# The bias of the output projection: four transposes of a repeated column in place of a matmul with one row

## The chip, the cores and the metric

The kernel runs on one core of one Trainium2 chip. The metric is the device time of one execution in microseconds (us), lower is better. The kernel before ran three times: 2654.74, 2656.70 and 2658.29 us, median 2656.7 us. A further execution was recorded by the hardware profiler; all rows below are from it.

## What is computed

Four sequences of 1024 rows with 1024 features go through a selective state-space layer and then through a feed-forward layer with routed experts. In short, all in float32:

```python
# state space: x is layer-normed and is the gate z; ctx goes in
x_in  = einsum('ed,bld->bel', in_proj_w, ctx)          # 1024 x 512 weights
u     = silu(causal_conv4(x_in) + conv_b)
dt_lo, Bm, Cm = split(einsum('ke,bel->bkl', x_proj_w, u))   # 32, 16, 16 rows
delta = softplus(dt_proj_w @ dt_lo + dt_proj_b)
state = state * exp(delta * A) + (delta * u) * Bm      # 16 states a channel, over 1024 steps
y     = (sum over states of state * Cm + D * u) * silu(z)
x     = x + y.T
# feed-forward, on the layer-normed x (called xn)
gate, top = top_k(softmax(xn.flatten() @ switch_w.T + switch_b), 2)
o   = sum over the 2 experts of gate * (gelu(xn_head @ w1 + b1) @ w2 + b2)
x   = x + (xn + o) @ w3.T + b3
```

The change is about the last line's `+ b3`, a vector of 1024 values that is added to every row.

## The kernel before, in words

**Stages.** The channels are cut in J = 8 blocks of P = 128, the time in TH = 2 halves of T = 512. One step of the scan is one block of channels over one half: 16 steps a batch (the names use g for the step), and each step has eight slots of two states. In a slot ScalarE makes dA = exp(delta * A) (L1100), VectorE multiplies du by B (L1299) and scans the two states (L1326) into one of three pairs of h buffers, GpSimd multiplies them with C (L799), and TensorE adds the products up by eight transposes into the bank yT (L862, `sum_pair`). Four more transposes of u * D open that sum (L957), four transpose the gate's block (L944, "zT"), the four matmuls of in_proj make the input ten steps ahead (L833), x_proj comes twice a batch (L845), and L854 makes the input of the softplus.

**What sets the order.** Each engine has a program of its own, written out from one table: `Schedule` holds for batch b and slot t the extra pieces of work. The feed-forward layer of batch b - 1 is done while batch b is scanned: its logits (L976), the transposes of the rows (L905), the experts (L918, L928), and the output tiles. The last batch's feed-forward part has nothing beside it and makes the tail.

**Output tiles.** An output tile is 128 rows by QD = 512 features: 16 tiles a batch (two halves uu of the rows, two halves dh of the features, four row blocks k), 64 in all. In the scan a tile is four "tile" pieces (part 0 to 3) of two blocks of the contraction each, put in slots 56 to 79 and 99 to 126 of the batch behind; within a slot they follow `sum_pair`. In the tail the 16 tiles stand one behind the other. Before part 0, TensorE waits until the bank (one of two, F0 and F1, in turn) was read out, and then writes the bias into it; then it waits for its share of w3 and adds the eight blocks (L995). The float32 matmul of 128x512 appears as two passes in the trace. VectorE adds the residual while it reads the bank (L1285), and SyncE stores the tile (L708) and loads the next residual (L701).

**The bias before.** At setup b3 is loaded as one row of 1024 values into partition B3 = 64 of the tile dtw (L555), whose partitions 0 to 32 hold dt_proj and its bias, and 96 to 127 hold rows of B and C. For a tile, one matmul multiplies row 64 of a tile of ones (1 x 128) by 512 values of that row (1 x 512), with start=True (L991). The loads of the small constants are thirteen DMAs on SyncE's queue (L559), all counted on one semaphore; ScalarE and GpSimd wait for it before their first work, TensorE before x_proj.

Of the kernel before, what the change touches and what calls it, by code (L numbers as in the profile page):

```python
# [11 lines left out]
P = 128  # L12
# [4 lines left out]
J = DI // P  # L17
# [10 lines left out]
SWL = DI // SD  # L28
QD = 512
NQ = DI // QD  # L30
B3 = 64
RA = 4
RH = 3
SLOTS = PAIRS
# [215 lines left out]
def build(nc, x, ctxT, w_inT, conv_w, conv_b, x_projT, dt_projT, dt_b, A_log, D, sw, sw_b,  # L250
# [4 lines left out]
    with ExitStack() as ctx:  # L255
        def sb(name, shape, dt=F32):
            return ctx.enter_context(nc.sbuf_tensor(name, shape, dt))
# [11 lines left out]
        ident = sb("ident", [P, P])  # L269
        ones = sb("ones", [P, P])  # L270
# [4 lines left out]
        dtw = sb("dtw", [P, DI])  # L275
# [3 lines left out]
        Av = sb("Av", [P, J * N])  # L279
        b1c = sb("b1c", [P, E])  # L280
        b2c = sb("b2c", [P, E])
        swb = sb("swb", [P, E])

        ctxs = sb("ctxs", [P, DK, T])
# [62 lines left out]
        dense = ctx.enter_context(nc.psum_tensor("dense", [P, 8, T], F32))  # L347
# [89 lines left out]
        def bank_of(b, *name):  # L437
            return PLAN.use[(b, *name)][0]

        def count(b, *name):  # L440

            return PLAN.use[(b, *name)][1]
# [19 lines left out]
        def f_index(b, k):  # L462
            return 2 * TB * b + k

        def logit_batch(b, k):
            return b - 1 if k >= TB else b
# [4 lines left out]
        def sw_tile(b, k, i):  # L471

            m = SWL * (k % TB) + i
            if k < TB:
                return ring_b[m % RING_B], sw_b_loaded[m % RING_B], 1 + 16 * (b * len(range(m % RING_B, SWL * TB, RING_B)) + m // RING_B + 1)
            if b < NB:
                r = m % RING_A
                return ring_a[r], sw_a_loaded[r], 1 + 16 * ((b - 1) * len(range(r, SWL * TB, RING_A)) + m // RING_A + 1)
            return ring_t[m % RING_T], sw_t_loaded[m % RING_T], 1 + 16 * (m // RING_T + 1)
# [4 lines left out]
        def row_of(b, what, k):  # L484

            if (b, what, k) in PLAN.fill:
                i = PLAN.fill[(b, what, k)]
                return row[:, i % 2, :], row_loaded[i % 2], 1 + 16 * (i // 2 + 1)
            i = k - TB - 2 if what == "logits" else 2 + k
            return tail_rows[i], tail_row_loaded[i], 1 + 16  # L490
# [18 lines left out]
        def w3_of(b, uu, dh, c):  # L509
            if b < NB:  # L510
                return w3h, w3_loaded[c], 1 + 16 * (2 * NQ * (b - 1) + NQ * uu + dh + 1)
            if dh == 0:
                return w3h, w3_loaded[c], 1 + 16 * (2 * NQ * (b - 1) + 1)
            return w3_tail, w3_tail_loaded[c], 1 + 16

        @block.sync
        def _(sync):
            e = sync
# [24 lines left out]
            with nc.allow_non_contiguous_dma(reason="small weights, once"):  # L543
                for dst, src in (
                    (cw[:], conv_w.rearrange("(j p) k -> p j k", p=P)),
                    (cb[:], conv_b.rearrange("(j p) -> p j", p=P)),
                    (xpw[:], x_projT.rearrange("(j p) k -> p j k", p=P)),
                    (Dv[:], D.rearrange("(j p) -> p j", p=P)),
                    (Av[:].rearrange("p (j n) -> p j n", n=N), A_log.rearrange("(j p) n -> p j n", p=P)),
                    (b1c[0:HD], b1.rearrange("e f -> f e")),  # L550
                    (b1c[HD:P], b1.rearrange("e f -> f e")),
                    (b2c[0:HD], b2.rearrange("e d -> d e")),
                    (b2c[HD:P], b2.rearrange("e d -> d e")),
                    (swb[:], sw_b.partition_broadcast(P)),
                    (dtw[B3:B3 + 1], b3.rearrange("(o d) -> o d", o=1)),  # L555
                    (dtw[0:DR], dt_projT),
                    (dtw[DR:DR + 1], dt_b),
                ):
                    e.dma_start(dst, src).then_inc(const_loaded, 16)  # L559
# [264 lines left out]
        def _(pe):  # L824
            e = pe
# [54 lines left out]
            def slot(b, t):  # L880
                st, q = divmod(t, SLOTS)
                g, c = STEPS * b + st, TH * b + st // J
                th, j = divmod(st, J)
                for what, *a in PLAN.slots[b][t]:
# [8 lines left out]
                    elif what == "turn":  # L893
                        uu, k, i = a
                        bank = bank_of(b, *name)
# [7 lines left out]
                        for n in range(J // 2):  # L903
                            d = (J // 2) * i + n
                            mm = e.transpose(dense[:, bank, n * P:(n + 1) * P], rows[:, d * P:(d + 1) * P], ident[:])  # L905
                        mm.then_inc(tr_done, 1)
                    elif what == "hidden":
# [7 lines left out]
                        for i in (0, 1):  # L915
                            bank = bank_of(b, *name, i)
# [3 lines left out]
                    elif what == "expert_out":  # L920
                        uu, hp = a
                        bank = bank_of(b, *name)
# [4 lines left out]
                        for i in (0, 1):  # L927
                            mm = e.matmul(dense[HD * i:HD * i + HD, bank, :], w2s[:], hs_of(b, hp)[:, i, :],  # L928
                                          start=True, stop=True)
# [21 lines left out]
                if b < NB:  # L951
                    if q == 2:
# [3 lines left out]
                        for k in range(TB):  # L956
                            e.matmul(yT[:, k, :], uD[:, k * P:(k + 1) * P], ident[:], is_transpose=True,  # L957
                                     start=(k == 0), stop=False, skip_group_check=True)
# [3 lines left out]
                for what, *a in PLAN.slots[b][t]:  # L962
                    if what == "logit":
                        k, i = a
                        f = f_index(logit_batch(b, k), k)
                        first = k % TB == 0 and i == 0
                        if i == 0:
                            e.wait_ge(norm_done, 1 + f + 1)
                        if first:
                            e.wait_ge(evac[F2], 1 + count(b, "logits", k // TB))  # L970
                        weights, loaded, value = sw_tile(b, k, i)
                        e.wait_ge(loaded, value)
                        rows = row_of(b, "logits", k)[0]
                        for n in range(SD // 32):
                            lo = i * SD + 32 * n
                            mm = e.matmul(dense[32 * n:32 * n + 32, F2, 0:32 * E], rows[:, lo:lo + 32],  # L976
                                          weights[:, :, 32 * n:32 * n + 32],
                                          start=first, stop=(k % TB == TB - 1 and i == SWL - 1))
                        mm.then_inc(sw_used, 1)
                    elif what == "tile":  # L980


                        uu, dh, k, part = a
                        bank = bank_of(b, "tile", uu, dh, k)
                        w3, loaded, value = w3_of(b, uu, dh, part)
                        if part == 0:
                            if dh == 0 and k == 0:
                                last = ("expert_out", uu, J - 1)
                                e.wait_ge(evac[bank_of(b, *last)], 1 + count(b, *last) + 1)
                            e.wait_ge(evac[bank], 1 + count(b, "tile", uu, dh, k))  # L990
                            e.matmul(dense[:, bank, :], ones[B3:B3 + 1, :], dtw[B3:B3 + 1, dh * QD:(dh + 1) * QD],  # L991
                                     start=True, stop=False)
                        e.wait_ge(loaded, value)
                        for d in range(J // W3C * part, J // W3C * (part + 1)):
                            mm = e.matmul(dense[:, bank, :], xT_of(b, uu)[:, d, k * P:(k + 1) * P], w3[:, d, :],  # L995
                                          start=False, stop=(d == J - 1))
                        mm.then_inc(part_done, 1)
            turns(slot)

        @block.scalar  # L1000
# [443 lines left out]
```

## Time and profile before

| | |
|---|---|
| runs shown, us | 2654.74, 2656.70, 2658.29 |
| profiled execution, us | 2655.29 |
| its span, us | 2653.5 |
| mean granted TensorE clock | 0.849 of 2.4 GHz |
| TensorE matmul (PE) busy | 1998.5 us, 75% |
| TensorE weight load (PEld) busy | 1083.4 us, 41% |
| VectorE (DVE) busy | 2238.3 us, 84% |
| ScalarE (ACT) busy | 1542.8 us, 58% |
| GpSimd (POOL) busy | 1446.2 us, 55% |

The span is the profiled part of the execution; 1.8 us lie around it. Engines run at the same time, each through its own list, and wait for each other by semaphores. PE and PEld overlap: the weights of the next pass are loaded while the present one runs. Durations of matmuls overlap their successors in the record, since passes are pipelined; what a pass costs is therefore read from the start of one group to the start of the next, and not from its length. A busy share is an average over stages with different limits.

### The profile page before, as it was taken

How to read it: one execution, taken by the hardware profiler on the slowest of the kernel's cores; microseconds unless marked ns; L12 is line 12 of the kernel's file. 1: busy time of each engine (PE TensorE's matmuls, PEld its weight loads, DVE VectorE, ACT ScalarE, POOL GpSimd, SP SyncE). 2: the span in 40 equal slices, each digit the busy share in tenths (PEclk: the TensorE clock that was granted, in tenths of full speed). 3: DMA queues.
4: the chain of work that ended last, by engine and by line, in shares of the span. 5: the costliest groups of instructions: out<-in, count | busy, mean ns of one | idle time of the engine just before them, and what ended most of it. 6: DMA issues, size and time to landing. Idle time of an engine off the chain costs nothing.

```text
span 2653.5 us, 29890 instructions
## 1 busy us (share of the span) xinstructions
PE 1998.5 (75%) x9360; PEld 1083.4 (41%) x9360; DVE 2238.3 (84%) x2928; ACT 1542.8 (58%) x2225; POOL 1446.2 (55%) x990
## 2 busy tenths in 40 slices
PE   5365566666676898899675798899675797895899
PEld 2143334443443344344443344344443344442233
DVE  4399999999999889998999889998999999994300
ACT  2366555555666757855676746954666858852400
POOL 0177666666765556555775555555675666662000
PEclk9677777778787899899787899899787998997899
DMA  3401241445552364466461274465560274557311
GB/s 107 179 27 59 73 164 49 158 159 191 183 182 72 112 222 135 135 210 199 160 226 67 89 242 140 127 197 191 181 223 26 78 231 146 170 184 267 150 57 62
DMA packets 200050, 386.78 MB, mean 146 GB/s; under 512 B 30642, under 2 KB 96178, under 8 KB 199892
## 3 DMA queue, kind: packets, MB, share of 16 engines
q1 hardware_dynamic: 199892, 384.87, 43.3%
q8 instruction: 75, 1.23, 0.2%
q14 instruction: 83, 0.68, 0.1%
HBM read 350.73 MB, written 34.08 MB: 145 GB/s over the span
## 4 chain that ended last, share of the span: by engine, by line
PE 37%; issue 22%; DVE 22%; ACT 9%; POOL 6%; DMA 1%; SPq 1%; DVEq 0%; ACTq 0%; POOLq 0%
PE dense L995 13%; DVE h L1326 10%; PE dense L862 8%; PE dense L833 5%; POOL h L799 5%; DVE dense L1299 5%; ACT dA L1100 3%; DVE u L1191 2%; PE dense L845 2%; PE dense L991 2%; PE dense L928 2%; PE dense L976 2%; PE dense L918 1%; ACT L1059 1%; ACT hs L1162 1%
## 5 line engine op out<-in xcount | busy, mean ns | idle before, releaser
L799 POOL TENSOR_TENSOR h<-h,Cb 128x1024 f32<-128x1024 f32 x512 | 1208.0, 2359 | 473.6 <-DVE h L1326 450.0
L1100 ACT ACTIVATE dA<-delta,Av 128x512 f32<-128x512 f32 x1024 | 702.9, 717 | 514.0 <-DVE h L1326 511.9
L862 PE MATMUL dense<-ident,h 128*128 128x128 f32 x4096 | 635.1, 310 | 274.4 <-POOL h L799 272.9
L862 PEld LDWEIGHTS dense<-ident,h 128*128 128x128 f32 x4096 | 545.4, 161 | 450.0 <-POOL h L799 353.8
L1326 DVE TENSOR_TENSOR_SCAN h<-dA,state,dense 128x512 f32<-128x512 f32 x512 | 628.1, 1264 | 56.1 <-PE dense L862 33.8
L1299 DVE TENSOR_TENSOR dense<-dense,Bb 128x512 f32<-128x512 f32 x1024 | 653.3, 684 | 4.2 <-ACT dense L1055 2.1
L1326 DVE TENSOR_TENSOR_SCAN h<-dA,dense 128x512 f32<-128x512 f32 x512 | 597.6, 1204 | 24.0 <-PE dense L862 11.3
L995 PE MATMUL dense<-w3h,xT 128*128 128x512 f32 x832 | 391.6, 604 | 0.0
L833 PE MATMUL dense<-ctxs,win 128*128 128x512 f32 x512 | 273.0, 684 | 31.2 <-DMA win<-in_w_inT 25.4
L854 PE MATMUL dense<-dtaug,dtw 33*128 33x512 f32 x128 | 104.1, 906 | 209.8 <-DVE u L1191 180.5
L793 POOL COPY state<-h 128x2 f32<-128x2 f32 x256 | 48.0, 188 | 382.0 <-DVE h L1326 380.5
L995 PEld LDWEIGHTS dense<-w3h,xT 128*128 128x128 f32 x832 | 146.9, 191 | 167.1 <-issue 167.1
L833 PEld LDWEIGHTS dense<-ctxs,win 128*128 128x128 f32 x512 | 110.8, 227 | 169.0 <-issue 138.4
L1191 DVE SCALAR_TENSOR_TENSOR u<-dense,cw,u 128x511 f32<-128x511 f32 (+2 forms) x192 | 140.5, 732 | 32.2 <-ACT u L1025 16.1
L1285 DVE TENSOR_TENSOR res<-dense,res 128x512 f32<-128x512 f32 x64 | 43.8, 685 | 122.8 <-PE dense L995 122.5
L1059 ACT ACT_TABLE_LOAD x112 | 143.7, 1283 | 2.0
L1055 ACT COPY dense<-du_s 128x512 f32<-128x512 f32 x64 | 37.6, 587 | 155.3 <-DVE dense L1299 133.3
L976 PE MATMUL dense<-sww,row 128*32 128x256 f32 x1336 | 115.3, 433 | 15.5 <-ACT row L1130 14.6
L854 PEld LDWEIGHTS dense<-dtaug,dtw 33*128 33x128 f32 x128 | 25.7, 250 | 240.9 <-issue 240.9
L928 PE MATMUL dense<-hs,w2s 128*64 128x512 f32 x224 | 74.6, 731 | 38.5 <-ACT hs L1162 38.2
L786 POOL TENSOR_TENSOR xt<-szT,xt 128x512 f32<-128x512 f32 x64 | 81.8, 1278 | 3.0 <-DVE szT L1243 3.0
L1162 ACT ACT_TABLE_LOAD x49 | 62.9, 1283 | 34.4 <-PE dense L918 34.0
(136 smaller groups left out, 1842.1 us busy)
## 6 DMA issues: line engine op xcount, KB each, us to landing
sww<-in_sw SPq DMA_DIRECT2D x170, 512.0 KB, 4.4
Bb<-bc_scratch SPq DMA_DIRECT2D x64, 512.0 KB, 4.5
Cb<-bc_scratch SPq DMA_DIRECT2D x64, 512.0 KB, 5.8
w3h<-in_sw SPq DMA_DIRECT2D x56, 512.0 KB, 7.5
w3h<-in_w3T SPq DMA_DIRECT2D x52, 512.0 KB, 4.7
row<-x_scratch SPq DMA_DIRECT2D x42, 512.0 KB, 4.7
win<-in_w_inT SPq DMA_DIRECT2D x64, 256.0 KB, 4.0
row<-in_x SPq DMA_DIRECT2D x32, 512.0 KB, 4.3
```

Of the source, the lines that this page charges most:

```text
L799: e.tensor_tensor(h[:, s:s + 2, :], h[:, s:s + 2, :], Cb[:, 2 * q:2 * q + 2, :], ALU.mult).then_inc(prod_done, 1)
L833: mm = e.matmul(dense[:, bank, :], win[:, par, k, :], ctxs[:, k, :], start=(k == 0), stop=(k == DK - 1))
L854: e.matmul(dense[:, S, :], dtw[0:DR + 1, j * P:(j + 1) * P], dtaug[:], start=True, stop=True) \
L862: mm = e.matmul(yT[:, k, :], h[:, 2 * (q % RH) + i, k * P:(k + 1) * P], ident[:], is_transpose=True, start=False, stop=(q == PAIRS - 1 and ...
L928: mm = e.matmul(dense[HD * i:HD * i + HD, bank, :], w2s[:], hs_of(b, hp)[:, i, :], start=True, stop=True)
L976: mm = e.matmul(dense[32 * n:32 * n + 32, F2, 0:32 * E], rows[:, lo:lo + 32], weights[:, :, 32 * n:32 * n + 32], start=first, stop=(k % TB ...
L995: mm = e.matmul(dense[:, bank, :], xT_of(b, uu)[:, d, k * P:(k + 1) * P], w3[:, d, :], start=False, stop=(d == J - 1))
L1059: e.preload_act_table_set("natural_log_exp_and_others")
L1100: e.activation(dst, delta[:, st % 2, :], ACT.Exp, scale=Av[:, j * N + n:j * N + n + 1]).then_inc(dA_done, 1)
L1191: i = e.scalar_tensor_tensor(out=u[:, G % UR, s:T], in0=dense[:, bank, 0:T - s], scalar=cw[:, j, k:k + 1], in1=u[:, G % UR, s:T], op0=ALU. ...
L1299: e.tensor_tensor(duB[:, n % 2, :], du[:], Bb[:, n, :], ALU.mult).then_inc(duB_done, 1)
L1326: e.tensor_tensor_scan(h[:, 2 * (q % RH) + n % 2, :], decay, inflow, state[:, j * N + n:j * N + n + 1] if th else 0.0, ALU.mult, ALU.add) \
```

## The change

The row of b3 in dtw goes, and with it the constant B3. In its place a new tile b3c [128, 8] holds b3 by columns: partition p of column j is b3[128 j + p]. For a tile, TensorE now makes four transposes: column 4 dh + n, repeated 128 times along the free dimension, is the stationary operand, the identity is the moving one, and the result, 128 features in every one of the 128 rows, goes to columns 128 n to 128 n + 127 of the bank. The first has start=True; the others, and the matmuls of w3 behind them, add to the same bank.

```diff
-B3 = 64
...
+        b3c = sb("b3c", [P, J])
...
-                    (dtw[B3:B3 + 1], b3.rearrange("(o d) -> o d", o=1)),
+                    (b3c[:], b3.rearrange("(j p) -> p j", p=P)),
...
                             e.wait_ge(evac[bank], 1 + count(b, "tile", uu, dh, k))
-                            e.matmul(dense[:, bank, :], ones[B3:B3 + 1, :], dtw[B3:B3 + 1, dh * QD:(dh + 1) * QD],
-                                     start=True, stop=False)
+                            for n in range(QD // P):
+                                column = QD // P * dh + n
+                                e.matmul(dense[:, bank, n * P:(n + 1) * P], b3c[:, column:column + 1].broadcast_to([P, P]),
+                                         ident[:], is_transpose=True, start=(n == 0), stop=False, skip_group_check=True)
                         e.wait_ge(loaded, value)
                         for d in range(J // W3C * part, J // W3C * (part + 1)):
                             mm = e.matmul(dense[:, bank, :], xT_of(b, uu)[:, d, k * P:(k + 1) * P], w3[:, d, :],
-                                          start=False, stop=(d == J - 1))
+                                          start=False, stop=(d == J - 1), skip_group_check=True)
```

## Rows read from the trace of the kernel before

**Rows 1.** Page, part 4: the chain that ended last, shares of the span by line
```profile
PE dense L995 13%; DVE h L1326 10%; PE dense L862 8%; PE dense L833 5%; POOL h L799 5%; DVE dense L1299 5%; ACT dA L1100 3%; DVE u L1191 2%; PE dense L845 2%; PE dense L991 2%; PE dense L928 2%; PE dense L976 2%; PE dense L918 1%; ACT L1059
```
**Rows 2.** Busy time by stretch; x is instructions, first numbers are start:end and length
```profile
core 0: us, PE busy (x) PEld busy (x) DVE busy (x) ACT busy (x) POOL busy (x), PEclk, DMA share, GB/s
916.00:1030.00 114.00, 107.92 (x413) 57.99 (x412) 100.08 (x126) 61.91 (x92) 65.44 (x38) 0.97 0.57 191
1118.00:1240.00 122.00, 121.02 (x577) 58.72 (x576) 106.93 (x134) 65.74 (x98) 72.35 (x41) 1.00 0.57 182
1522.00:1634.00 112.00, 105.93 (x403) 56.91 (x403) 98.28 (x123) 59.95 (x88) 63.78 (x37) 0.97 0.58 193
1722.00:1844.00 122.00, 121.01 (x577) 58.87 (x577) 106.95 (x134) 65.74 (x98) 72.41 (x41) 1.00 0.57 182
2112.00:2206.00 94.00, 89.00 (x356) 47.83 (x354) 86.41 (x102) 55.79 (x79) 60.20 (x36) 1.00 0.62 202
2309.00:2412.00 103.00, 96.58 (x489) 48.72 (x487) 99.64 (x121) 52.88 (x73) 67.46 (x33) 0.99 0.52 168
2520.00:2653.50 133.50, 130.22 (x290) 52.00 (x288) 11.82 (x17) 0.00 (x0) 0.00 (x0) 1.00 0.17 59
```
**Rows 3.** Timeline of the tail, TensorE: start us, us, engine, line, operands
```profile
2617.69 1.12 PE L991 MATMUL dense<-dtw,ones 1*128 1x512 f32 x2
2618.74 7.13 PE L995 MATMUL dense<-Cb,u 128*128 128x512 f32 x16
2625.81 1.12 PE L991 MATMUL dense<-dtw,ones 1*128 1x512 f32 x2
```
**Rows 4.** Timeline of a tile stretch of batch 1, TensorE
```profile
957.85 3.60 PE L995 MATMUL dense<-w3h,xT 128*128 128x512 f32 x8
961.28 1.04 PE L862 MATMUL dense<-ident,h 128*128 128x128 f32 x8
962.25 1.12 PE L991 MATMUL dense<-dtw,ones 1*128 1x512 f32 x2
963.30 3.70 PE L995 MATMUL dense<-w3h,xT 128*128 128x512 f32 x8
966.93 1.12 PE L854 MATMUL dense<-dtaug,dtw 33*128 33x512 f32 x2
...
978.15 0.60 PE L944 MATMUL dense<-ident,xz 128*128 128x128 f32 x4
978.58 1.04 PE L862 MATMUL dense<-ident,h 128*128 128x128 f32 x8
```
**Rows 5.** VectorE's waits from 1118 to 1240 us: us in total, times, longest
```profile
DVE h L1326 <- ACT dA L1100: 6.5, 1, 6.5
DVE h L1326 <- PE dense L862: 5.9, 3, 3.0
DVE delta L1221 <- ACT delta L1049: 2.4, 1, 2.4
```
**Rows 6.** Timeline of the setup, SyncE's issues
```profile
11.05 0.87 SPq L559 DMA_DIRECT2D cb<-in_conv_b  x1
20.51 0.34 SPq L559 DMA_DIRECT2D dtw<-in_b  x1
```
**Rows 7.** Groups by line and form: busy us, mean ns, idle before
```profile
L1299 DVE TENSOR_TENSOR dense<-dense,Bb 128x512 f32<-128x512 f32 x1024 | 653.3, 684 | 4.2 <-ACT dense L1055 2.1
L944 PE MATMUL dense<-ident,xz 128*128 128x128 f32 x256 | 41.4, 285 | 21.2 <-DVE delta L1221 20.4
L944 PEld LDWEIGHTS dense<-ident,xz 128*128 128x128 f32 x256 | 28.2, 143 | 44.0 <-issue 43.9
L1389 DVE TENSOR_TENSOR sww<-hs,hot 128x512 f32<-128x512 f32 x12 | 8.3, 692 | 0.7
```
**Rows 8.** Busy time by stretch, as rows 2: a slow stretch, then lone transposes
```profile
942.50:949.20 6.70, 6.62 (x15) 3.31 (x15) 6.57 (x9) 4.11 (x7) 6.17 (x6) 0.57 1.03 373
...
2473.58:2478.33 4.75, 4.75 (x24) 3.65 (x24) 3.84 (x18) 3.26 (x7) 0.00 (x0) 0.64 0.98 366
2478.54:2479.73 1.19, 1.19 (x8) 0.81 (x8) 1.15 (x2) 0.94 (x2) 0.00 (x0) 1.00 1.03 399
```

## The prediction

> **What bounds the kernel now.** I start with the chain of waits of the whole span [rows 1]. Its shares by line put TensorE's w3 products (L995) first with 13%, then VectorE's scan (L1326), and the bias matmul L991 itself holds 2%. Two per cent of 2653.5 us is some 53 us; one bias costs 1.05 us from its start to that of the next matmul [rows 3], so about 50 of the 64 lie on the chain. That is why I look at the places of L991 and not at its busy share.
>
> The second view is the table by stretch [rows 2]: the six stretches of the scan in which output tiles are made (two in each of the batches 1, 2 and 3), and the tail from 2520 us on. The reader is to compare PE's and DVE's busy time with the length. In the tail PE is busy 130.2 of 133.5 us and DVE 11.8: PE is the bound alone. In the four stretches of batches 1 and 2 PE has 107.9 of 114 us, 121.0 of 122, 105.9 of 112 and 121.0 of 122, while DVE, which sets the pace of a scan without tiles, is idle for 13.9, 15.1, 13.7 and 15.1 us. So there too PE is mostly the bound. In batch 3 PE has 89.0 of 94 us with 7.6 us of idle DVE, and then 96.6 of 103 with only 3.4. ACT and POOL have room everywhere.
>
> The third view says whom DVE waits for in one such stretch [rows 5]: 5.9 us for L862 (TensorE's sum of a pair, which frees an h buffer), and 6.5 and 2.4 us for ScalarE's dA and delta. ScalarE's turn comes behind x_proj (L845) and the product L854, both on TensorE, so these waits too are at least in part PE's lateness, one engine further on.
>
> **What the change removes.** At each of 64 tiles one matmul with one row of contraction, which the trace shows as two passes (L991 x2). In the tail a tile repeats every 2625.81 - 2617.69 = 8.12 us [rows 3]. Without a bias its 16 passes would take 16 x 0.429 = 6.86 us; the 0.429 is read where nothing of the kind stands around: L995 x8 from 957.85 to 961.28 is 3.43 us [rows 4]. So the bias costs 8.12 - 6.86 = 1.26 us, which is more than the 1.05 from its own start to the next: the seam shows as well before it (L862 x8 takes 0.97 us when L991 follows, 961.28 to 962.25) and behind it (L995 x8 then takes 3.63 instead of 3.43, of which a part is due to the L854 that follows) [rows 4].
>
> **What it adds on TensorE.** Four transposes of 128 columns into the same bank, weights first, just as L862, L944 and L957 do. Four of L944 between L995 and L862 take 978.58 - 978.15 = 0.43 us [rows 4], and L995 ahead of them and L862 behind show no seam. All this at the full clock. So the sum for a tile is 1.26 - 0.43 = 0.83 us less on PE.
>
> That the weights are one column read 128 times has no row on TensorE. The bounds: nothing extra, which gives the 0.43; or the weight load no longer hides behind the product before it, 143 + 285 = 428 ns each [rows 7], 1.71 us for four, which is 0.45 us more than now. A gain over the 0.43 I exclude, since the number of columns is the same. The nearest row is of another engine: DVE's multiply by a broadcast operand (L1389) takes 692 ns against 684 for one with plain operands (L1299) [rows 7]. I take nothing extra.
>
> **Setup.** The load of b3 as one row had an issue of 0.34 us; b3c has the shape and the pattern of cb, whose issue took 0.87 us [rows 6]. Two more loads of the same group come behind it on SP, then the rows and the next w_in tiles, and ACT, POOL and (for x_proj) PE wait for the whole group. All are delayed by 0.53 us, and nothing covers it, because ACT's first tap stands behind that wait. The bounds are 0 (the issue overlaps with landings) and some 1.5 us (the issue, and 1024 small elements on the way, which I guess at twice the issue's difference). I take 0.5 us.
>
> **What it moves.** No instruction changes its order: four transposes stand where the matmul stood, on PE, and the same waits (evac of the bank, w3_loaded) stand ahead of them or behind. The DVE, ACT and POOL lists are untouched. The 0.8 us earlier end of a tile wakes DVE's L1285 and SP's store, and in the tail these have room: DVE is busy 11.8 of 133.5 us.
>
> **Sum, tail.** 16 tiles x 0.83 = 13.3 us, all on the path.
>
> **Sum, scan.** 48 tiles, eight in a stretch: at most 8 x 0.83 = 6.6 us a stretch. DVE's idle time caps it, since DVE can't be shortened otherwise: 6.6 us is below 13.9, 15.1, 13.7, 15.1 and 7.6; in the last stretch the cap is 3.4, and as TensorE has 6.4 us to spare there I count 1.4. That is 5 x 6.6 + 1.4 = 34.4 us at most. At least it is 0, if ACT and POOL set the same waits. Between these I choose two thirds, 23 us: PE is full in the stretches, which speaks for the whole; but over half of the waits in [rows 5] (8.9 of 14.8 us) end on ScalarE, whose own work between PE and DVE doesn't shrink, and a wait gives back only what was gained since the one before it.
>
> **The result.** 13.3 + 23 - 0.5 = 35.8 us off the profiled execution's 2655.3 us gives 2619.5. The median of the runs shown, 2656.7, is 1.4 us above that execution, so I give 2621 us.
>
> **A rule against it.** Of 32 transposes that stood alone at 2473.58 to 2479.73 us, with no other matmul among them, the first 24 ran at a mean granted clock of 0.64 and the last 8 at 1.00 [rows 8], so the clock rose to 2.4 GHz while TensorE did nothing but transposes. And the tile stretches, full of L862's transposes, have 0.97 to 1.00 [rows 2]. The Trainium skill, "TensorE: Matmul & The Clock Gate", Part 4 (PE-mode transpose), says the contrary: the full clock doesn't engage for transpose mode, as it doesn't count as PE-busy in the same way. By that rule the kernel would get more uncounted work and could lose clock (second rival); by the row it can't.
>
> **Rivals.**
> 1. *Tail only.* The scan's waits are set by others too (dA by ScalarE, delta by its chain), and end as late as before: 2655.3 - 13.3 + 0.5 = 2642.5, 2644 against the median. For it: the 8.9 us in [rows 5]. Against: L991 is on the chain some 50 times, when the tail has 16.
> 2. *The clock falls, slower.* In the tail, the transposes would break the run of multiplying passes 16 times, and TensorE would drop to 1.2 GHz. Where the clock was down, 942.5 to 949.2 us, it was 0.57 [rows 8], that is almost all at 1.2 GHz, and there everything on PE takes twice as long. The tail without the bias matmul is 16 x 7.29 = 117 us at the full clock; each tenth of it at the lower level costs 11.7 us, so from three tenths the whole gain is gone, and with all of it at 1.2 GHz the time is 2621 + 117 = 2738. Against: rows 8 and 2 as above.
> 3. *The weight load of a repeated column is in the open, slower.* 0.45 us more a tile instead of 0.83 less: 7.2 in the tail, two thirds of 21.6 in the scan, 0.5 in the setup: 22 us, 2679 against the median. It decides from 0.83 / 4 = 0.21 us of extra time for each load.
> 4. *No gain.* The seams of rows 4 come from something else than the single row (the first product into a bank, say) and stand around the transposes as well: each seam of some 0.2 us on both sides and between the passes takes back the most of 0.83; about 2655.
>
> **Chances.** Forecast 0.64, reaching from all of the scan's 34.4 us (2609.5) to a third of them (2632.4); tail only 0.20 (2644); no gain 0.07; slow load 0.05; clock 0.04. The range from 2609 to 2645 holds the first two. About 0.2%, 5.3 us, is what a measurement of this kernel can tell from no change. Faster by more: the first two cases and a little of the fourth, 0.85. Within it: 0.06. Slower: 0.09.
>
> **What would show it.** In the changed kernel's timeline of the tail a tile should repeat every 7.29 us, with four transposes in 0.43 us, and L995 in 3.43 us per eight passes with no seam; clock 1.00. Each tile stretch should be shorter by 4 to 5 us and DVE's idle time in it smaller by as much, the named waits for L862 first. The first scan should start 0.5 us later. A tail period near 8.1 or above, a PEld time for the new line over 0.2 us, or a granted clock under 0.95 in the tail would each refute a step, and unchanged stretches with a shorter tail would make it rival 1.

## The result, and the profile after

The changed kernel took 2620.5 us in the median of four runs (2614.8 to 2621.0), the kernel before 2656.1 (2654.7 to 2658.3, four runs): ratio 0.986, 95% interval 0.9843 to 0.9877. Run again on another chip beside thirteen runs of the kernel before it gave 0.9862 (0.9825 to 0.9900), 2616.7 against 2654.1 us, with single runs from 2610.4 to 2625.8 (the kernel before beside it: 2643.8 to 2658.5). The forecast was 2621. Two executions of one experiment below (the delayed kernel before), at 3012 and 9517 us, were in a slow state of the chip and are left out of its ratio.

The chain of waits of the changed kernel, where L993 is the new bias and L997 the w3 products (answers to [rows 1]):

```profile
DVE h L1328 12%; PE dense L997 11%; PE dense L862 7%; POOL h L799 5%; DVE dense L1301 5%; PE dense L833 4%; ACT dA L1102 3%; DVE u L1193 3%; PE dense L845 2%; PE dense L928 1%; ACT L1061 1%; PE dense L918 1%; DVE szT L1245 1%; PE dense L976
```

The w3 products have given up the first place to VectorE's scan, and of the bias no line is left among the large ones.

The timeline of the tail, TensorE (start us, us; answers to [rows 3]):

```profile
2595.03 0.60 PE L993 MATMUL dense<-ident,b3c 128*128 128x128 f32 x4
2595.46 7.03 PE L997 MATMUL dense<-Cb,u 128*128 128x512 f32 x16
2602.33 0.60 PE L993 MATMUL dense<-ident,b3c 128*128 128x128 f32 x4
```

A tile repeats after 2602.33 - 2595.03 = 7.30 us; the four transposes take 0.43 us from start to start and the 16 passes 6.87. The seams are gone. The same in a tile stretch of batch 1 (answers to [rows 4]):

```profile
951.61 3.60 PE L997 MATMUL dense<-w3h,xT 128*128 128x512 f32 x8
955.04 1.04 PE L862 MATMUL dense<-ident,h 128*128 128x128 f32 x8
955.92 0.60 PE L993 MATMUL dense<-ident,b3c 128*128 128x128 f32 x4
956.35 3.60 PE L997 MATMUL dense<-w3h,xT 128*128 128x512 f32 x8
```

L862 ahead of the bias now takes 0.88 us in place of 0.97, and the bias 0.43 in place of 1.05.

The weight load of the repeated column, from the groups by line and form (busy us, mean ns; answers to [rows 7]):

```profile
L993 PE MATMUL dense<-ident,b3c 128*128 128x128 f32 x256 | 38.9, 275 | 0.0
L944 PEld LDWEIGHTS dense<-ident,xz 128*128 128x128 f32 x256 | 28.5, 144 | 44.0 <-issue 43.8
L993 PEld LDWEIGHTS dense<-ident,b3c 128*128 128x128 f32 x256 | 30.5, 138 | 13.8 <-issue 13.8
```

138 ns for the repeated column and 144 for a plain tile: repetition costs nothing.

**Where the time went.** The first start of L957 marks each step of the scan, so the two profiled executions can be laid side by side, in us. Steps 7 to 11 hold the first tile stretch of a batch, steps 12 to 15 the second; what stands behind L957 of the last step is called the rest, and the 16 tiles are in it.

| stretch | before | after | difference |
|---|---|---|---|
| to the first step | 118.58 | 121.69 | +3.11 |
| batch 0 (no tiles) | 547.12 | 542.64 | -4.48 |
| batch 1, steps 0 to 6 | 257.34 | 255.00 | -2.34 |
| batch 1, steps 7 to 11, tiles | 193.88 | 188.13 | -5.75 |
| batch 1, steps 12 to 15, tiles | 153.40 | 152.20 | -1.20 |
| batch 2, steps 0 to 6 | 256.93 | 248.15 | -8.78 |
| batch 2, steps 7 to 11, tiles | 193.85 | 187.85 | -6.00 |
| batch 2, steps 12 to 15, tiles | 153.39 | 152.11 | -1.28 |
| batch 3, steps 0 to 6 | 245.68 | 248.40 | +2.72 |
| batch 3, steps 7 to 11, tiles | 170.63 | 168.32 | -2.31 |
| batch 3, steps 12 to 14, tiles | 97.67 | 96.21 | -1.46 |
| the rest, 16 tiles in it | 265.00 | 252.34 | -12.66 |
| span | 2653.47 | 2613.04 | -40.43 |

The tile stretches give 18.0 us and the tail 12.7. The other rows sum to -9.8, and the largest of them, 8.8 us, stands in a stretch that holds not one output tile. That was the open question. (Batch 0's 4.5 us are scatter: over the profiles of all the kernels below it takes 542.6 to 543.0 us in four and 545.8 to 547.5 in ten, with either bias in both groups.) Three of its rows in the busy time by stretch, of the kernel before:

```profile
core 0: us, PE busy (x) PEld busy (x) DVE busy (x) ACT busy (x) POOL busy (x), PEclk, DMA share, GB/s
1116.92:1270.32 153.40, 140.06 (x650) 69.55 (x649) 137.51 (x170) 82.27 (x123) 89.77 (x51) 0.96 0.59 191
1270.32:1527.25 256.93, 180.72 (x960) 108.16 (x960) 245.01 (x340) 176.25 (x257) 162.34 (x134) 0.79 0.39 137
1527.25:1721.10 193.85, 166.38 (x736) 86.85 (x734) 175.76 (x221) 133.51 (x184) 109.12 (x60) 0.92 0.53 171
```

and of the changed kernel:

```profile
1107.46:1259.66 152.20, 136.25 (x666) 71.90 (x665) 137.57 (x170) 82.22 (x123) 89.73 (x51) 0.94 0.60 193
1259.66:1507.81 248.15, 171.43 (x961) 102.39 (x961) 243.90 (x339) 176.37 (x256) 162.44 (x134) 0.83 0.40 140
1507.81:1695.66 187.85, 157.18 (x749) 88.16 (x747) 175.33 (x221) 133.47 (x184) 109.23 (x60) 0.94 0.55 178
```

In the middle rows the work is the same (DVE 245.0 and 243.9 us), but TensorE's mean clock is 0.79 in the one and 0.83 in the other.

**Why the second tile stretch gives little.** VectorE's waits in steps 12 to 15 of batch 1 after the change (us in total, times, longest; answers to [rows 5]):

```profile
DVE h L1328 <- ACT dA L1102: 6.0, 1, 6.0
DVE h L1328 <- PE dense L862: 3.1, 2, 1.9
DVE res L1287 <- PE dense L997: 2.7, 1, 2.7
DVE delta L1223 <- ACT delta L1051: 1.6, 1, 1.6
```

L862 fell from 5.9 to 3.1, delta from 2.4 to 1.6 and dA from 6.5 to 6.0 against [rows 5]: 4.1 us gone. But a wait is new: VectorE comes to its turn of adding the residual of the last tile 2.7 us before the tile is through. By steps, 12 to 14 take 110.4 us in place of 114.4, the 4 us that I had expected, and step 15 takes 41.8 in place of 39.0. In step 15 TensorE's clock fell for 6.8 us, 14 us behind its start, where it had stayed up in the kernel before. The same pieces of work in the kernel before and in the changed one:

```profile
1247.50 1.88 PE L995 MATMUL dense<-w3h,xT 128*128 128x512 f32 x4
1249.22 3.60 PE L833 MATMUL dense<-ctxs,win 128*128 128x512 f32 x8
...
1234.88 3.62 PE L997 MATMUL dense<-w3h,xT 128*128 128x512 f32 x4
1238.29 3.86 PE L833 MATMUL dense<-ctxs,win 128*128 128x512 f32 x8
```

and the busy time by stretch there, before and after:

```profile
1245.50:1252.30 6.80, 5.73 (x20) 3.10 (x21) 6.05 (x6) 4.39 (x6) 6.23 (x4) 1.00 0.84 284
1232.00:1238.80 6.80, 5.68 (x13) 3.45 (x14) 6.06 (x6) 4.43 (x6) 6.26 (x4) 0.50 0.95 321
```

At a granted clock of 0.50, which is 1.2 GHz, the four passes take 1238.29 - 1234.88 = 3.41 us in place of 1.72, and the last tile is through 26.9 us behind the start of step 15 in place of 24.1. In batch 2 the same happens more weakly (step 15: 40.7 us in place of 39.0). All seven profiles with transposes in the scan's tiles have it. So in step 15 the clock took back 2.8 and 1.7 us of what the transposes gave. It isn't a matter of transposes: of the kernels below, the one without any bias falls to 1.2 GHz there as well (step 15: 40.7 us), and the one with 128 rows in the bias matmul doesn't (39.0). Nor is a cheaper bias needed: two profiles below with the single row have a longer step 15 in one batch each (the delayed kernels before, 40.3 us in batch 1 and 40.7 in batch 2). Why the clock falls in the one and not in the other was not tried.

The first stretches are not purely the bias either: the kernel with 128 rows gained 4.6 us in steps 7 to 11 of batch 1, more than the 8 x 0.41 = 3.3 us by which its bias is cheaper there.

**Setup.** The new load (answers to [rows 6]):

```profile
20.24 0.43 SPq L559 DMA_DIRECT2D b3c<-in_b  x1
```

Its issue took 0.43 us, 0.09 more than the row's and half of the 0.87 that I had taken from cb. ScalarE's first instruction behind the group started at 24.18 us.

### The profile page after: what moved, and what is told of

It is laid out like the page before. It is cut to its first block, busy times and chain, and to the rows that moved or that the text cites. A ratio compares the mean times of both kernels' runs of the same rounds, so it can differ in the third digit from the quotient of the medians.

```text
span 2613.0 us, 30146 instructions
## 1 busy us (share of the span) xinstructions
PE 1947.3 (75%) x9488; PEld 1099.9 (42%) x9488; DVE 2237.0 (86%) x2928; ACT 1544.3 (59%) x2225; POOL 1446.3 (55%) x990
## 4 chain that ended last, share of the span: by engine, by line
PE 30%; DVE 25%; issue 25%; ACT 9%; POOL 6%; DMA 1%; SPq 1%; DVEq 1%; ACTq 0%; POOLq 0%
DVE h L1328 12%; PE dense L997 11%; PE dense L862 7%; POOL h L799 5%; DVE dense L1301 5%; PE dense L833 4%; ACT dA L1102 3%; DVE u L1193 3%; PE dense L845 2%; PE dense L928 1%; ACT L1061 1%; PE dense L918 1%; DVE szT L1245 1%; PE dense L976 1%; ACT hs L1164 1%
## 5 line engine op out<-in xcount | busy, mean ns | idle before, releaser
L862 PE MATMUL dense<-ident,h 128*128 128x128 f32 x4096 | 651.1, 315 | 280.7 <-POOL h L799 278.5
L862 PEld LDWEIGHTS dense<-ident,h 128*128 128x128 f32 x4096 | 556.6, 164 | 458.2 <-POOL h L799 369.7
L997 PE MATMUL dense<-w3h,xT 128*128 128x512 f32 x832 | 389.3, 601 | 0.0
L833 PE MATMUL dense<-ctxs,win 128*128 128x512 f32 x512 | 267.2, 672 | 31.4 <-DMA win<-in_w_inT 25.0
L854 PE MATMUL dense<-dtaug,dtw 33*128 33x512 f32 x128 | 104.0, 904 | 207.9 <-DVE u L1193 179.1
L997 PEld LDWEIGHTS dense<-w3h,xT 128*128 128x128 f32 x832 | 148.9, 194 | 129.3 <-issue 129.3
L833 PEld LDWEIGHTS dense<-ctxs,win 128*128 128x128 f32 x512 | 108.8, 222 | 165.0 <-issue 138.1
L1287 DVE TENSOR_TENSOR res<-dense,res 128x512 f32<-128x512 f32 x64 | 43.9, 686 | 111.1 <-PE dense L997 110.9
L854 PEld LDWEIGHTS dense<-dtaug,dtw 33*128 33x128 f32 x128 | 25.8, 251 | 239.2 <-issue 239.2
L976 PE MATMUL dense<-sww,row 128*32 128x256 f32 x1336 | 111.2, 420 | 16.1 <-ACT row L1132 16.1
L928 PE MATMUL dense<-hs,w2s 128*64 128x512 f32 x224 | 71.3, 699 | 41.3 <-ACT hs L1164 40.7
L756 POOL TENSOR_TENSOR du_s<-delta,u 128x512 f32<-128x512 f32 x64 | 81.6, 1276 | 1.1 <-DVE delta L1223 1.1
```

What stands on the lines that cost most here:

```text
L833: mm = e.matmul(dense[:, bank, :], win[:, par, k, :], ctxs[:, k, :], start=(k == 0), stop=(k == DK - 1))
L854: e.matmul(dense[:, S, :], dtw[0:DR + 1, j * P:(j + 1) * P], dtaug[:], start=True, stop=True) \
L862: mm = e.matmul(yT[:, k, :], h[:, 2 * (q % RH) + i, k * P:(k + 1) * P], ident[:], is_transpose=True, start=False, stop=(q == PAIRS - 1 and ...
```

## The experiments

**The change again, its two halves, and no bias at all.** All four ran on one chip, beside thirteen runs of the kernel before with a median of 2654.1 us.

*The changed kernel again.*

> The changed kernel once more, as the measure for the others and for its own scatter. Four executions lay at 2614.8, 2620.5, 2620.6 and 2621.0 us. If the scatter comes from where the clock's changes fall against the work, again values from 2614 to 2622 us; if the 2614.8 was a single outlier, all within 1 us of 2620.6.

Four runs: 2618.6, 2625.8, 2614.8 and 2610.4 us. The spread is wider than even the first expectation allowed. Its profiled execution has the same tail (its 16 tiles and what follows take 119.86 us from the first w3 product on, as in the first profile) and the same 248.2 us in steps 0 to 6 of batch 2.

*Transposes in the tail alone, and in the scan alone.* Both loads of b3 stand at setup, so that the two are alike in it. The first has `b == NB` in this place, the second `b < NB`:

```diff
-                            for n in range(QD // P):
-                                column = QD // P * dh + n
-                                e.matmul(dense[:, bank, n * P:(n + 1) * P], b3c[:, column:column + 1].broadcast_to([P, P]),
-                                         ident[:], is_transpose=True, start=(n == 0), stop=False, skip_group_check=True)
+                            if b == NB:
+                                for n in range(QD // P):
+                                    column = QD // P * dh + n
+                                    e.matmul(dense[:, bank, n * P:(n + 1) * P], b3c[:, column:column + 1].broadcast_to([P, P]),
+                                             ident[:], is_transpose=True, start=(n == 0), stop=False, skip_group_check=True)
+                            else:
+                                e.matmul(dense[:, bank, :], ones[B3:B3 + 1, :], dtw[B3:B3 + 1, dh * QD:(dh + 1) * QD],
+                                         start=True, stop=False, skip_group_check=True)
```

> The four transposes in the 16 tiles of the tail alone, the matmul with one row in the 48 tiles of the scan; both loads of b3 at setup. Theory (the path's share as predicted: 13.1 us from the tail, some 23 from the scan): 2656 - 13 + 0.5 = 2643 to 2644 us. Rival (the scan gave little, and the rest of the gain came from elsewhere, such as the other place of the constants or the order of waits): near 2625 us.

> The four transposes in the 48 tiles of the scan alone, the matmul with one row in the tail; both loads of b3. Theory: the tail's period is 8.12 us as before and the whole is 2620.5 + 13 + 0.5 = 2634 us; together with the kernel of the tail alone the two gains add up to that of the change within 3 us. Rival (gains that overlap): the two sum to clearly more or less than 35.5 us.

Tail alone: 2644.9 us, ratio 0.9970 (0.9955 to 0.9985), 9.2 us off. Scan alone: 2631.3 us, ratio 0.9910 (0.9879 to 0.9940), 22.8 us off. Both lie within 3 us of the theory, and the rival (the scan gave little) is out. The two sum to 32.0 us, where the whole change gave 37.4 on that chip: 5.4 us apart, more than the 3 I had allowed, though the intervals are 8 and 16 us wide. The stretches are cleaner than the totals: the tail's 16 tiles and what follows take 132.1 us with the matmul with one row, in the kernel before and in the scan alone, and 119.86 with transposes, 12.2 us less. And steps 0 to 6 of batch 2 take 256.92 us with the tail alone and 248.20 with the scan alone, so 8.7 of the scan's 22.8 us stand where there is no tile.

*No bias.* b3 is left out of the sum:

```diff
-                            for n in range(QD // P):
...
                         for d in range(J // W3C * part, J // W3C * (part + 1)):
                             mm = e.matmul(dense[:, bank, :], xT_of(b, uu)[:, d, k * P:(k + 1) * P], w3[:, d, :],
-                                          start=False, stop=(d == J - 1), skip_group_check=True)
+                                          start=(d == 0), stop=(d == J - 1), skip_group_check=True)
```

> No bias at all: b3 is left out of the sum, the first w3 matmul opens the bank; the load of b3c stays. It prices the four transposes. Theory: the tail's period falls from 7.30 to 16 x 0.429 = 6.86 us, 7 us in all; of the scan's 48 x 0.44 = 21 us about half to two thirds return; 2600 to 2604 us. Rival (in the scan TensorE is no longer the bound once the bias costs 0.43 us, and scans and dA set the pace): only the tail's 7 us, 2613 us.

2614.6 us, only 2.0 below the changed kernel. That is near the rival's number, but not by its sum. The profile's busy time by stretch, batch 2:

```profile
1261.66:1517.79 256.13, 178.90 (x958) 106.30 (x958) 243.79 (x339) 176.16 (x256) 161.89 (x134) 0.79 0.39 136
1517.79:1704.55 186.76, 157.36 (x722) 86.04 (x720) 175.79 (x222) 133.41 (x184) 109.44 (x61) 0.92 0.56 178
1704.55:1855.57 151.02, 133.31 (x634) 68.19 (x633) 138.50 (x171) 82.19 (x123) 89.67 (x51) 0.94 0.60 196
```

The tiles gave a little more: 186.76 and 151.02 us, another 1.1 each below the changed kernel's (some 5 in all six tile stretches, half of what the theory asked for), and the tail's tiles took 113.4 us against 119.9, 6.5 less. But steps 0 to 6 are back at 256.1 us, with the clock at 0.79. Eight microseconds returned in a stretch that the edit doesn't touch.

**Setup.** *Both loads, the second read by nobody.* The kernel before, with the load of b3c added to the group.

> The kernel before with the load of b3c added to the group at setup (14 loads in place of 13), and read by nobody. Theory (the load costs its issue, 0.5 us, once): 2656.5 to 2657 us, the first VectorE tap 0.5 to 0.6 us later. Rival (the first scan step starts 3.1 us later in the profile of the change because of this load): about 2659 us, and the first step again 3 us later.

2656.7 us against 2655.0, ratio 1.0004 (0.9993 to 1.0015), which fits the cost of the issue and is not at odds with no cost. But the interval reaches to 4 us, so it doesn't exclude the rival's 3 either, and that profile did start the first step late, at 122.16 us. *The load behind those of B and C*, with a semaphore of its own:

```diff
-                    (b3c[:], b3.rearrange("(j p) -> p j", p=P)),
...
             load_xz(0, 0, 0)
+            with nc.allow_non_contiguous_dma(reason="small weights, once"):
+                e.dma_start(b3c[:], b3.rearrange("(j p) -> p j", p=P)).then_inc(b3_loaded, 16)
...
+                            if (b, uu, dh, k) == (1, 0, 0, 0):
+                                e.wait_ge(b3_loaded, 1 + 16)
```

> The changed kernel with the load of b3c taken out of the group at setup and issued behind the loads of B and C, with a semaphore of its own for which TensorE waits once before the first output tile. Theory: the setup group is through at 23.3 us or before in place of 24.2, and the whole is 0.5 to 1 us below the changed kernel. Rival (the 3.1 us later first step are the load's doing): 3 us below it.

2619.4 us, ratio 0.9859 (0.9842 to 0.9875). The group is through at 23.31 us, 0.87 before the changed kernel's, but the first step came at 121.76 us, no earlier. The time is the changed kernel's within the spread. What lies between shows in TensorE's first groups of in_proj, here of the kernel before:

```profile
27.10 8.60 PE L833 MATMUL dense<-ctxs,win 128*128 128x512 f32 x16 [2.53 <-DVE u L1191]
54.59 8.52 PE L833 MATMUL dense<-ctxs,win 128*128 128x512 f32 x16 [5.19 <-DMA win<-in_w_inT]
```

of the changed kernel:

```profile
27.72 10.18 PE L833 MATMUL dense<-ctxs,win 128*128 128x512 f32 x16 [3.13 <-DVE u L1193]
57.59 8.92 PE L833 MATMUL dense<-ctxs,win 128*128 128x512 f32 x16 [5.22 <-DMA win<-in_w_inT]
```

and of the one with the late load:

```profile
26.85 8.67 PE L835 MATMUL dense<-ctxs,win 128*128 128x512 f32 x16 [2.49 <-DVE u L1197]
54.53 10.20 PE L835 MATMUL dense<-ctxs,win 128*128 128x512 f32 x16 [5.27 <-DMA win<-in_w_inT]
```

The same 16 passes take 8.5 or 10.2 us, as TensorE's clock came up sooner or later in them, and where the long one falls differs from kernel to kernel.

**What makes the seam.** The kernel before, with 128 rows of contraction in the bias matmul in place of one (a wrong constant takes the place of b3):

```diff
-                            e.matmul(dense[:, bank, :], ones[B3:B3 + 1, :], dtw[B3:B3 + 1, dh * QD:(dh + 1) * QD],
+                            e.matmul(dense[:, bank, :], ones[:], xpw[:].rearrange("p j k -> p (j k)"),
                                      start=True, stop=False)
```

> The kernel before with the bias matmul of 128 rows of contraction in place of one: ones (128x128) times 512 columns of x_proj's weights, so a wrong constant takes the place of b3. Theory (the seams of 0.2 us on either side belong to the matmul with a single row, whose weights are not loaded behind the pass before): the tail's period is 18 x 0.429 = 7.72 us, and the bias costs 0.86 in place of 1.26. Rival (the seams belong to the first pass into a bank): 8.12 us as before.

Its timeline in the tail:

```profile
2615.12 1.02 PE L991 MATMUL dense<-xpw,ones 128*128 128x512 f32 x2
2615.97 7.03 PE L995 MATMUL dense<-Cb,u 128*128 128x512 f32 x16
2622.84 1.02 PE L991 MATMUL dense<-xpw,ones 128*128 128x512 f32 x2
```

The period is 7.72 us and the two passes cost 0.85: the theory, to the hundredth. The matmul with 128 rows, 128 times the work, is 0.40 us cheaper than the one with a single row. One execution took 2635.8 us. By stretches against the kernel before, the tile stretches give 11.7 us in place of the change's 18.0, and the tail's tiles 6.0 in place of 12.2, so some half of the gain of the change is to be had without a transpose.

The single row is not the only shape with seams. L854, with 33 rows, still has them in this kernel:

```profile
1229.91 1.12 PE L854 MATMUL dense<-dtaug,dtw 33*128 33x512 f32 x2
1230.96 1.09 PE L862 MATMUL dense<-ident,h 128*128 128x128 f32 x8
1231.89 1.02 PE L991 MATMUL dense<-xpw,ones 128*128 128x512 f32 x2
1232.75 1.88 PE L995 MATMUL dense<-w3h,xT 128*128 128x512 f32 x4
```

From its start to the next, L854's two passes take 1.05 us, as the single row's did, and the two with 128 rows 0.86. The first part of the seam goes wider still. At the full clock a pass of the w3 products takes 0.43 us to the next start, and 0.52 where one with 33 rows (L854) or one with 128 rows and 32 columns (L976) comes next; a transpose of L862 takes 0.11 us, and 0.20 ahead of L976 or of L918 with its 64 rows. Ahead of the bias with 128 rows nothing is added. So the 0.09 us in front stands where a pass with fewer rows or columns follows a full one, the other parts were seen at 1 and 33 rows, and none of it is special to a single row. How the engine comes to it, by the weight load as the theory has it or otherwise, no run here shows.

**GpSimd adds the bias in the tail.** The late load, transposes in the scan, and in the tail:

```diff
+                    elif what == "tile_out" and b == NB:
+                        uu, dh, k = a
+                        n = part_index(b, uu, dh, k, 0) // W3C
+                        e.wait_ge(b3b_loaded, 1 + 16)
+                        e.wait_ge(res_loaded[n % 2], 1 + 16 * (n // 2 + 1))
+                        e.tensor_tensor(res[:, n % 2], res[:, n % 2], dA[:, dh, :], ALU.add).then_inc(res_biased, 1)
```

dA is free by then and holds b3 repeated over the partitions; VectorE waits for res_biased, and TensorE opens the bank with the first w3 product.

> A version that may beat both: the late load of b3c, the transposes in the scan's tiles, and in the tail no bias on TensorE: GpSimd, idle there, adds a repeated b3 to the residual before VectorE adds the product. Theory: the tail's period is 6.86 us; 16 x 0.43 = 7 us below the kernel with the late load alone, about 2613 us. Rival (the chain load of the residual, GpSimd, VectorE, store, next load becomes longer than two tiles of 13.7 us, or GpSimd slows VectorE): a period of 7.3 us or above and no gain.

2608.75 us, four runs within 1.1 us, ratio 0.9823 (0.9807 to 0.9840). The tiles and what follows take 113.4 us. This is the fastest version: 46 us below the kernel before, about 11 below the late load alone, of which 6.5 us are the tail's tiles. The other microseconds stand mostly (3.9) between the start of the last scan step and the first tile, a piece that took 132.2 us here, 132.5 in the changed kernel and 136.1 with the late load; why it was long there stays open. The chain through GpSimd in its timeline:

```profile
2581.76 1.26 POOL L833 TENSOR_TENSOR res<-res,dA 128x512 f32<-128x512 f32 x1 [5.81 <-DMA res<-x_scratch]
2583.05 0.69 DVE L1306 TENSOR_TENSOR res<-dense,res 128x512 f32<-128x512 f32 x1 [6.17 <-POOL res L833]
2588.65 1.27 POOL L833 TENSOR_TENSOR res<-res,dA 128x512 f32<-128x512 f32 x1 [5.63 <-DMA res<-x_scratch]
2589.91 0.69 DVE L1306 TENSOR_TENSOR res<-dense,res 128x512 f32<-128x512 f32 x1 [6.18 <-POOL res L833]
```

VectorE's turns are 2589.91 - 2583.05 = 6.86 us apart, TensorE's pace, but in these two it is GpSimd's add that ends last (in the next it is the w3 products), so a still shorter tile might meet this chain.

*The same with the load of b3c moved into batch 0's scan:*

> As the kernel with GpSimd's bias in the tail, with the load of b3c moved on from the setup into the first batch's scan (SyncE's slot 100). Theory (the setup lost time wherever this load stood in it): the first scan step begins at 118.6 us as in the kernel before, in place of 120.1 to 121.7, and the whole is 1.5 to 3 us lower, 2606 to 2607 us. Rival (the first step scatters with the clock and not with the load): no difference from 2608.8 us.

2609.9 us (2602.5 to 2613.0), ratio 0.9836 (0.9808 to 0.9863), first step at 120.92 us: the rival. With the group free of the new load the first step began at 118.6 to 121.8 us in seven profiles of this study (before 118.58, late load 121.76, this one 120.92; mean 120.0), with it at 120.7 to 124.1 in six of seven, and at 119.5 in the seventh (the delayed change, below; mean 121.5). These overlap, and the means are 1.5 us apart.

**The eight microseconds in batch 2.** The theory formed after these runs: whether TensorE's clock drops from 2.4 to 1.2 GHz during the expert work of step 5 depends on where the work lies against the clock's changes ahead of it. Two constants' statistics on VectorE, 1.4 us, shift what follows:

```diff
+                if b == 2 and t == 0:
+                    e.wait_ge(const_loaded, 1 + 16 * CONSTS)
+                    e.wait_ge(lgr_done, 4)
+                    for i in (0, 1):
+                        e.bn_stats(lgm[:, i, 0:6], xpw[:].rearrange("p j k -> p (j k)")).then_inc(pad_done, 1)
+                    e.wait_ge(pad_done, 1 + 2)
```

> The kernel before with 1.4 us of needless work on VectorE (two statistics of 512 constants) at the start of batch 2. It only shifts what follows against the times at which TensorE's clock changes. Theory (steps 0 to 6 of batch 2 take 248.2 us where the clock stays at 2.4 GHz during the expert work of step 5, and 255 to 257 us where it drops, and a shift of the start decides): this kernel's steps 0 to 6 of batch 2 take 248 us and the 1.4, in place of 256.9; the whole is 7 us below the kernel before, about 2648 us. Rival (the bias matmuls or their absence in the tiles ahead decide in another way, such as through backlog): 256.9 + 1.4 us, and the whole 1 to 2 us above the kernel before.

> The changed kernel with the same 1.4 us on VectorE at the start of batch 2. Theory: the favourable place is lost, steps 0 to 6 of batch 2 take 255 to 258 us in place of 248.2, and the whole is about 2620 + 8, 2626 to 2630 us. Rival (the transposes themselves keep the clock up): 248.2 + 1.4 us, and 2621 to 2622 us.

The delayed change: 255.67 us in steps 0 to 6 of batch 2 and 2625.1 us in all, ratio 0.9899 (0.9869 to 0.9930), against 0.986 without the delay. 7.5 us came of 1.4, as the theory says; the total is 1 us short of the expected range, and single runs of the changed kernel reach it too (2625.8), so here the stretch says more than the total. The delayed kernel before: 256.21 us, ratio 1.0001 (0.9985 to 1.0017). That is a miss. Its batch 1 had run differently ahead of it (steps 12 to 15 took 155.5 us in place of 153.4), so step 5 fell to another place than planned, with the clock's rise 2.96 us behind its start and not 1.2. The last run put the delay so close that nothing could take the shift back (t == 37 in place of 0):

> The kernel before with the 1.4 us of needless VectorE work put close ahead of step 5 of batch 2 (slot 37), so that nothing between can take the shift back. In the profiles so far the clock's rise nearest to the start of step 5 comes 1.1 to 1.2 us behind it where steps 5 and 6 are short (37.3 and 34.8 us), and 2.0 to 3.0 us behind it where they are long (40.4 to 40.8 and 38.3 to 39.2); in the kernel before it comes 2.6 us behind. Theory (the place alone decides): with the work 1.4 us later the rise comes 1.2 us behind, steps 5 and 6 take 37.3 + 34.8 or near, some 7 us less than before, though the kernel has more work and the bias matmuls of before; the whole near 2649 us in such executions. Rival (the transposes of the tiles ahead are needed): 40.6 + 39.2 us and 2657 us.

Its busy time by stretch in steps 5 and 6, and in 6.5 us within step 5:

```profile
1450.33:1487.74 37.41, 26.10 (x116) 13.13 (x114) 36.61 (x51) 34.62 (x46) 22.84 (x18) 0.86 0.39 141
1487.74:1523.37 35.63, 30.87 (x128) 15.67 (x127) 33.59 (x47) 26.95 (x37) 22.86 (x18) 0.98 0.30 96
1463.40:1469.90 6.50, 6.22 (x27) 3.22 (x28) 6.50 (x9) 6.43 (x8) 5.32 (x6) 1.00 0.07 7
```

The same of the kernel before:

```profile
1460.50:1467.00 6.50, 5.58 (x13) 3.45 (x14) 6.50 (x9) 6.43 (x8) 5.32 (x6) 0.50 0.02 5
...
1447.48:1488.08 40.60, 27.99 (x116) 14.59 (x115) 36.72 (x51) 35.05 (x47) 22.82 (x18) 0.79 0.36 130
1488.08:1527.25 39.17, 34.53 (x129) 17.66 (x128) 33.72 (x47) 26.98 (x38) 22.84 (x18) 0.88 0.26 88
```

13 us behind the start of step 5 the clock is at 1.2 GHz in the kernel before and at 2.4 with the delay, in the same work. Steps 5 and 6 take 37.4 + 35.6 us in place of 40.6 + 39.2: 6.7 us less, near the forecast (37.3 + 34.8). What it does to one piece of work, L833 of that step, before and with the delay:

```profile
1463.18 5.56 PE L833 MATMUL dense<-ctxs,win 128*128 128x512 f32 x8
```

```profile
1464.61 3.60 PE L834 MATMUL dense<-ctxs,win 128*128 128x512 f32 x8
```

The whole kernel, with 1.4 us more to do and the bias matmuls of before, is faster, if by little: 2651.7 against 2655.1 us, ratio 0.9988 (0.9978 to 0.9998). The forecast was near 2649; steps 12 to 15 of the same batch gave back 2.5 us (155.9 in place of 153.4).

## Why the prediction was right, point by point

- **0.83 us a tile, the tail's 13.3 us.** Right: the period went from 8.12 to 7.30 us, which is 13.1 us in 16 tiles. (The 12.2 us of the stretch counted from the first w3 product leave out the first bias.) That the seam belongs to the matmul with one row and not to the first pass into a bank, which I had only read off two places, is shown by the matmul with 128 rows (0.85 us in place of 1.26); the 33 rows of L854 keep it, so it is not a matter of the single row alone.
- **Nothing extra for the repeated column.** Right: 138 ns a load against 144.
- **Two thirds of the scan's 34.4 us, 23.** The tile stretches gave 18.0 us in the profile. This is the term that was too large, by 5 us, and mostly in the second stretches: 1.2 to 1.5 us each where I had expected 4 to 5. In batches 1 and 2 steps 12 to 14 gave 4.0 and 3.0 us, and step 15 took back 2.8 and 1.7, as the clock fell to 1.2 GHz in it and the last tile was late for VectorE's turn at L1287. Without that the term would be about 22.5, an estimate from these steps. The two thirds themselves were a choice between bounds, and no run shows the reason given for them. The first stretches gave 5.8, 6.0 and 2.3.
- **That the total still fitted** is owed in part to 8.8 us which the sum doesn't contain. In both profiles of the changed kernel batch 2 lies where the clock doesn't drop in step 5. Without that stroke of luck, 2655.3 - 18.0 - 12.7 + 3.1 of the setup is 2627.7 us. The range would have held this too. These sums are of the profiled execution, 2614.8 us, the fastest of its four; the median was not profiled, though the other profile, at 2618.6 us, has the same 248.2 us in that stretch.
- **Setup, 0.5 us.** The group came through 0.6 us late (24.18 against 23.56 us by ScalarE's first instruction), but not for the reason given: the issue took 0.43 us and not cb's 0.87, so only 0.09 of it is the issue, and that the number fits is luck. The first step came 3.1 us later, and how much of that is the load is not settled: first steps with and without it overlap, a kernel with the load alone added is slower by 0.04%, with an interval that holds no change and 3 us as well, and taking it out of the setup gained nothing that can be measured.
- **The rivals.** *Tail only* is out: the scan alone gives 22.8 us, some 14 of them without batch 2's clock. *Slow load* is out, by the 138 ns. *No gain* is out; the seams are gone with the matmul of one row. *The clock falls* is out for the tail, where I had placed it: it stays at 1.00 with the transposes in it, as rows 8 suggested and against the rule of the Trainium skill, "TensorE: Matmul & The Clock Gate", Part 4 (PE-mode transpose), quoted there. In the second tile stretches it did fall, for 6.8 us of step 15 in batch 1 (0.50 where it had been 1.00), though not through the transposes, as the kernel without a bias shows. And the clock decided 8 us, in a stretch I had not looked at, and in favour.

## What to carry to other kernels

A matmul with a single row of contraction is not a cheap one: here it cost 1.26 us for 512 float32 columns at the full clock, against 0.85 with all 128 rows and 0.43 as four transposes, and the part of it that its own duration doesn't show is in the neighbours. Two passes with 33 rows took as long as the two with a single one (1.05 us), and a full pass ahead of one with fewer rows or columns took 0.09 us more. Price an instruction by the period with and without it. When TensorE swings between its two clocks, a small edit can win or lose several times its own size somewhere else (here 7.5 us from a shift of 1.4), in a stretch that it doesn't touch as in one that it does; compare stretch by stretch from a fixed mark, and call a difference in a stretch that the edit doesn't touch by its name before it is booked to the edit.

## What was not expected of the hardware

The clock's choice in one step hung on about a microsecond. In the profiles of these kernels, steps 5 and 6 took 72.1 to 73.0 us when the clock's rise nearest to the start of step 5 came 1.1 to 1.3 us behind it, and 78.4 to 80.1 us when it came 2.0 to 3.0 us behind. Of the 28 passes through batches 1 and 2 in fourteen profiles, 7 are of the first kind, all in batch 2, and 21 of the second, with none between. What lies between, and whether the spread of single runs (2610 to 2626 us for the changed kernel on one chip, 2644 to 2659 for the kernel before) comes of the same, was not tried.
